# A fused sequence and product-key expert kernel: half of GpSimd's products moved ahead of the weights, two list buffers, the first quad's activations in step 0, and the last norms on VectorE

## What is computed

```
# layer 1: a gated recurrence over the sequence
delta = softplus(x Wdelta'), decay = exp(-delta * sigmoid(log_a))
state_t = decay_t * state_(t-1) + sigmoid(x Wselect') * tanh(x Win')
x = layernorm(x + (sigmoid(x Wgate') * state) Wout')

# layer 2: product-key experts, 8 heads, 2 x 32 keys, 1024 experts
xn = batchnorm(x) * gamma + beta;  q = xn w_q';  sim[p] = q[p] . keys   (p = 0, 1)
sx, ix = top8(sim[0]);  sy, iy = top8(sim[1])
scores, pk = top8(all sums sx + sy);  idx = (32 ix + iy)[pk]
o = gelu(x . key_in[idx]) * softmax(scores)
x = layernorm(x + sum over heads and k of o * key_out[idx])
```

## Time and profile before

| | us |
|---|---|
| median of 3 runs | 490.32 |
| lowest, highest | 487.49, 490.91 |
| the profiled execution: its time | 490.44 |
| the profiled execution: its span | 488.5 |
| DVE busy | 432.3 (88%) |
| PE busy | 359.3 (74%) |
| ACT busy, POOL busy | 245.4, 243.5 (50% each) |

### The profile page before, as it was taken

One profiled execution on the slowest core, in us unless ns is written; L12 is line 12 of the kernel. 1 busy time (PEld: TensorE's weight loads), 2 busy tenths in 40 slices (PEclk: granted clock), 3 DMA queues, 4 the chain that ended last, 5 costly groups with the idle time before them and its releaser, 6 DMA issues.

```text
span 488.5 us, 23430 instructions
## 1 busy us (share of the span) xinstructions
PE 359.3 (74%) x9713; PEld 266.5 (55%) x9713; DVE 432.3 (88%) x2701; ACT 245.4 (50%) x402; POOL 243.5 (50%) x341
## 2 busy tenths in 40 slices
PE   5979858137877778778777887687688778687565
PEld 3445544015545466447655674467356747487555
DVE  2458986999999869999999999989999999999993
ACT  2897664354555534364556445545464456242233
POOL 1023350453529461828382969262929483969030
PEclk9979956767595977797599768877797598867579
DMA  8900000000000000000000000000000000000001
GB/s 241 192 3 1 1 1 0 1 1 3 4 2 5 3 3 4 5 2 5 25 5 3 3 26 3 5 3 26 3 4 4 25 5 3 4 26 4 3 25 44
DMA packets 7658, 8.90 MB, mean 18 GB/s; under 512 B 896, under 2 KB 6912, under 8 KB 7424
## 3 DMA queue, kind: packets, MB, share of 16 engines
q1 hardware_dynamic: 6976, 7.34, 5.8%
q10 hardware_dynamic: 576, 0.07, 0.1%
HBM read 5.31 MB, written 2.10 MB: 15 GB/s over the span
## 4 chain that ended last, share of the span: by engine, by line
DVE 37%; PE 29%; issue 12%; POOL 5%; ACT 3%; DVEq 0%; ACTq 0%; POOLq 0%
PE psum L993 10%; DVE idx L659 7%; PE psum L946 7%; PE psum L980 6%; DVE vals L651 5%; DVE picked L684 5%; DVE arena L718 5%; DVE arena L714 4%; PE psum L926 4%; DVE arena L708 3%; POOL arena L308 2%; DVE top L665 2%; PE psum L918 1%; DVE words L672 1%; POOL code L278 1%
## 5 line engine op out<-in xcount | busy, mean ns | idle before, releaser
L946 PE MATMUL psum<-arena 64*64 64x16 f16 x7424 | 88.3, 182 | 61.0 <-issue 55.3
L946 PEld LDWEIGHTS psum<-arena 64*64 64x64 f16 x7424 | 81.2, 120 | 79.1 <-issue 73.6
L993 PE MATMUL psum<-ko,arena 64*128 64x128 f32 x1024 | 92.2, 358 | 1.9 <-issue 1.9
L993 PEld LDWEIGHTS psum<-ko,arena 64*128 64x128 f32 x1024 | 88.8, 269 | 2.9 <-issue 2.5
L659 DVE FIND_INDEX8 idx<-vals,sims 128x8 uint32<-128x32 f32 x512 | 82.6, 186 | 0.0
L714 DVE TENSOR_TENSOR arena<-iota,listsT 128x4096 f16<-128x4096 f16 x32 | 75.5, 2359 | 0.0
L980 PE MATMUL psum<-x1T,trn 128*64 128x256 f32 x512 | 65.6, 410 | 13.1 <-ACT arena L461 12.4
L308 POOL TENSOR_TENSOR arena<-arena 128x512 f32<-128x512 f32 x56 | 69.6, 1276 | 0.0
L980 PEld LDWEIGHTS psum<-x1T,trn 128*64 128x64 f32 x512 | 35.1, 146 | 49.7 <-ACT arena L461 25.4
L256 POOL TENSOR_TENSOR cand<-vals 128x128 f32<-128x128 f32 x16 | 9.4, 587 | 104.5 <-DVE vals L651 104.5
L453 ACT ACTIVATE arena<-psum 128x1024 f32<-128x1024 f32 x29 | 29.5, 1017 | 60.8 <-PE psum L946 60.8
(11 more groups left out here) (126 smaller groups left out, 570.2 us busy)
## 6 DMA issues: line engine op xcount, KB each, us to landing
x<-in_L_attn_x_dram SPq DMA_DIRECT2D x8, 256.0 KB, 5.6
out_dram<-nat SPq DMA_DIRECT2D x7, 256.0 KB, 2.5
ko<-in_L_ffn_key_out_dram SPq DMA_DIRECT2D x2, 512.0 KB, 9.9
nat<-in_L_ffn_key_in_dram SPq DMA_DIRECT2D x2, 256.0 KB, 10.1
nat<-in_L_ffn_keys_dram SPq DMA_DIRECT2D x2, 128.0 KB, 5.5
out_dram<-nat SPq DMA_DIRECT2D x2, 128.0 KB, 1.7
nat<-in_L_attn_W_delta_dram SPq DMA_DIRECT2D x1, 64.0 KB, 2.8
nat<-in_L_attn_W_in_dram SPq DMA_DIRECT2D x1, 64.0 KB, 2.7
```

Source lines behind the costliest of these rows:

```text
L946: end = pe.matmul(psum[64 * e:64 * e + 64, at:at + NJ], hotx[rows, g, :, e], hotw[rows, part, g, :, e], start=(part == 0), stop=(part == 1))
L993: end = pe.matmul(y2[:, e, m % 2] if m < NS - 1 else y_last[:, e], gl[rows, m % GL, j, :], ko[rows, j, :], start=(j == 0), stop=(j == NJ - 1))
```

## The change

1. `weigh(m - 3)` on POOL is cut in two: its first two instructions stand between candidate_sums(m) and weights(m - 1), the other two stay behind weights(m - 1).
2. listsT has two buffers, used in turn; the copy into it waits for the one-hot matrices of two steps ago instead of those of the last step.
3. The first quad's expert inputs and gelus, of which 2 of 8 rounds stood ahead of step 0 on PE and the rest in step 1, move forward: round 0 on PE between the transposes of chunks 5 and 6, round 1 before scores(0), the rest behind scores(1), which is itself moved ahead of the step loop. On ACT gelus 0 to 3 stand before sims_out(1), gelus 4 and 5 behind it, 6 and 7 in step 1. signs(0) stands ahead of normed(2).
4. The last two parts' norm is one DVE instruction per 128 tokens (subtract the mean, multiply by the reciprocal deviation) instead of a DVE scale and an ACT activation.
5. In the tail DVE takes both_parts(1) before the statistics of the last but one quad, and POOL's last multiplication (L325) waits for one half less of the one-hot matrices (`hot_done` 31 instead of 32).

```diff
--- before.py
+++ after.py
@@ -117,7 +117,7 @@
-        listsT = sb("listsT", [P, 2, 4, P // 2], F16)
+        listsT = sb("listsT", [P, 2, 2, 4, P // 2], F16)
@@ -300,24 +300,26 @@
-            def weigh(m):
+            def weigh(m, first=0, last=4):
                 wait(pool, "p_evac", m * 2 + 2)
                 wait(pool, "gelu_done", (m // 2 + 1) * JR)
-                for r in range(4):
+                for r in range(first, last):
                     js = slice(4 * r, 4 * r + 4)
                     pool.tensor_tensor(gl[:, m % GL, js], pn[:, m % 3, js], gl[:, m % GL, js],
                                        ALU.mult).then_inc(s["a_done"], 1)
 
             for m in range(NS):
                 candidate_sums(m)
+                if m >= 3:
+                    weigh(m - 3, 0, 2)
                 if m >= 1:
                     weights(m - 1)
                 if m >= 3:
-                    weigh(m - 3)
+                    weigh(m - 3, 2, 4)
                 candidate_codes(m)
                 over_eighth(m)
             weigh(NS - 3)
-            pool.wait_ge(s["hot_done"], 2 * NS)
+            pool.wait_ge(s["hot_done"], 2 * NS - 1)
             pool.wait_ge(s["p_evac"], LAST)
@@ -440,8 +442,8 @@
             def lists_out(m):
                 wait(act, "lists_mm", m + 1)
-                wait(act, "hot_done", m * 2)
-                act.activation(listsT[:, :, :, :].rearrange("p h f t -> p f h t"),
+                wait(act, "hot_done", m * 2 - 2)
+                act.activation(listsT[:, m % 2].rearrange("p h f t -> p f h t"),
                                b_lists.rearrange("p (f h t) -> p f h t", f=4, h=2), ACT.Copy).then_inc(s["lists_evac"], 1)
@@ -452,10 +454,10 @@
-            def gelus(q):
+            def gelus(q, first=0, last=JR):
                 wait(act, "y2_mm", q * 2 - 4)
-                for r in range(JR):
-                    if r == 2:
+                for r in range(first, last):
+                    if r == 2 and q > 0:
                         signs(GELU_STEP[q])
@@ -482,17 +484,12 @@
-            def norm_out_half(u):
...
             normed(0)
             sims_out(0)
             normed(1)
+            gelus(0, 0, 4)
+            sims_out(1)
+            gelus(0, 4, 6)
             for m in range(NS):
...
                 low_halves(m)
+                if m == 0:
+                    signs(0)
...
-                if m + 1 < NS:
+                if 1 <= m < NS - 1:
                     sims_out(m + 1)
                 if m + 2 < NS:
                     normed(m + 2)
-                if m in GELU_STEP:
+                if m == GELU_STEP[0]:
+                    signs(m)
+                    gelus(0, 6)
+                elif m in GELU_STEP:
                     gelus(GELU_STEP.index(m))
...
             for u in range(2):
                 spread2_half(u)
-                norm_out_half(u)
@@ -801,13 +802,16 @@
-            def last_scales(u):
+            def last_out(u):
                 n = slice(2 * u, 2 * u + 2)
                 dve.wait_ge(s["sd2"], NCH + u)
                 dve.reciprocal(rstd2[:, n], rstd2[:, n]).then_inc(s["rstd2_done"], 1)
                 dve.wait_ge(s["rstd2_done"], NCH + u)
-                dve.scalar_tensor_tensor(out=nmr2[:, n], in0=mv2[:, n, 0], scalar=-1.0, in1=rstd2[:, n],
-                                         op0=ALU.mult, op1=ALU.mult).then_inc(s["nmr2_done"], 1)
+                dve.wait_ge(s["stored"], 16 * (NCH - 1))
+                for t in range(2 * u, 2 * u + 2):
+                    end = dve.tensor_scalar(outb[:, t, :], zf[:, t, :], mv2[:, t:t + 1, 0], rstd2[:, t:t + 1],
+                                            ALU.subtract, ALU.mult)
+                end.then_inc(s["out_done"], 1)
@@ -826,13 +830,13 @@
             both_parts(0)
             residual(NCH - 2)
+            both_parts(1)
             stats(NCH - 2)
-            both_parts(1)
             both_parts(2)
             scales(NCH - 2)
             for u in range(2):
                 last_residual(u)
-                last_scales(u)
+                last_out(u)
@@ -913,6 +927,11 @@
+                if c == 6:
+
+                    pe.wait_ge(s["x1T_evac"], 1)
+                    pe.wait_ge(s["w_evac"], 5)
+                    experts_in(0, 0, 1)
                 wait(pe, "bst_done", c + 1 - RING)
@@ -994,9 +1003,10 @@
-            pe.wait_ge(s["w_evac"], 5)
-            experts_in(0, 0, 2)
+            experts_in(0, 1, 2)
             scores(0)
+            scores(1)
+            experts_in(0, 2)
             for m in range(NS):
...
-                if m + 1 < NS:
+                if 1 <= m < NS - 1:
                     scores(m + 1)
-                if m in GELU_STEP:
-                    experts_in(GELU_STEP.index(m), 2 if m == GELU_STEP[0] else 0)
+                if m in GELU_STEP[1:]:
+                    experts_in(GELU_STEP.index(m))
```

More of the change, by code:

```diff
@@ L483, in spread2_half @@
                 act.activation(rstd2[:, n], mv2[:, n, 1], ACT.Sqrt, bias=eps[:, 0:1]).then_inc(s["sd2"], 1)
-            def norm_out_half(u):
-                act.wait_ge(s["nmr2_done"], NCH + u)
-                act.wait_ge(s["stored"], 16 * (NCH - 1))
-                for t in range(2 * u, 2 * u + 2):
-                    end = act.activation(outb[:, t, :], zf[:, t, :], ACT.Identity, bias=nmr2[:, t:t + 1],
-                                         scale=rstd2[:, t:t + 1])
-                end.then_inc(s["out_done"], 1)
             normed(0)
@@ L518, in _ @@
                     spread2(m // 2 - 2)
-                if m < NS - 1 and m not in GELU_STEP:
+                if 0 < m < NS - 1 and m not in GELU_STEP:
                     signs(m)
@@ L703, in spread @@
                 def spread(f, n):
-                    v = listsT[:, hf, f, :].rearrange("p (g s) -> p g s", s=2)
+                    v = listsT[:, m % 2, hf, f, :].rearrange("p (g s) -> p g s", s=2)
                     return v.unsqueeze(2).to_broadcast([P, 32, n, 2])
@@ L716, in hots_of @@
                 wait(dve, "hoty_done", m * 2 + hf + 1)
-                both = listsT[:, hf, 2:4, :].rearrange("p w (g s) -> p (w g) s", s=2).unsqueeze(2)
+                both = listsT[:, m % 2, hf, 2:4, :].rearrange("p w (g s) -> p (w g) s", s=2).unsqueeze(2)
                 dve.tensor_tensor(hotw[:, :, at].rearrange("p w g j s -> p w (g j s)"),
@@ L907, in _, with experts_in @@
                 weights(g)
+            def experts_in(q, first=0, last=JR):
+                tokens = x1T[:, q * CW:(q + 1) * CW].rearrange("d (m e p) -> d e m p", m=2, e=2)
+                for r in range(first, last):
+                    wait(pe, "gelu_done", q * JR + r - 1)
+                    for b in range(2):
+                        for e in range(2):
+                            end = pe.matmul(b_g[r % 2][64 * e:64 * e + 64, b * SW:(b + 1) * SW],
+                                            trn[:, 9 + r, 64 * b:64 * b + 64], tokens[:, e], start=True, stop=True)
+                    end.then_inc(s["g_mm"], 1)
             for c in range(NCH):
@@ L972, in quarters @@
                     end.then_inc(s["q_mm"], 1)
-            def experts_in(q, first=0, last=JR):
-                tokens = x1T[:, q * CW:(q + 1) * CW].rearrange("d (m e p) -> d e m p", m=2, e=2)
-                for r in range(first, last):
-                    wait(pe, "gelu_done", q * JR + r - 1)
-                    for b in range(2):
-                        for e in range(2):
-                            end = pe.matmul(b_g[r % 2][64 * e:64 * e + 64, b * SW:(b + 1) * SW],
-                                            trn[:, 9 + r, 64 * b:64 * b + 64], tokens[:, e], start=True, stop=True)
-                    end.then_inc(s["g_mm"], 1)
             def experts_out(m):
```

## The result

The changed kernel took 498.01 us (median of 4 runs, 496.42 to 500.02), beside 490.48 us for the kernel before on the same chip (4 runs, 487.49 to 490.91). The ratio is 1.0191, with an interval of 1.0144 to 1.0237: slower, and 1.4 us above the forecast of 496.6. The profiled execution took 499.16 us with a span of 497.4, where before it was 490.44 with 488.5.

A forecast was written before the change was run, and what follows sets the result against it. The kernel was taken as bound by DVE, PE close behind. Start +0.9, steps 3 and 4 -0.8, steps 5 to 14 +6.2, step 15 +1.1, tail -1.15 gave +6.25 on 490.44: 496.7, as median 496.6, range 486 to 501.

The forecast's parts named there:

- The sum: Whole kernel: all terms together add +6.25 us to the profiled 490.44, giving 496.7.
- the ten steps: Steps 5 to 14: DVE's floor rises to 48.96 us a pair and old waits vanish in it, +6.2 us.
- The blocked codes: DVE's L692, steps 3 to 15: waits for POOL's whole second product, 1.1 us a step, bounds nothing to 1.24.
- 14 us or more: Sign over the whole kernel: DVE's busy time would rise by some 14 us or more.
- Rival A: Codes on DVE aren't blocked, or go before the second product; tail's L325 may be harmless: 486.7 us, chance 0.22.
- Rival C: The copy L691 meets the second product and only its rest is paid, 0.3 to 0.5 a step: 491.3 us, chance 0.18.
- Rival B: DVE's new time isn't taken up, as lists and PE's queue come later too: +11 us, 501.5, chance 0.1.
- Steps 3 and 4: Waits in step 4 absorb both steps' 1.1 price; earlier signs start the one-hot matrices 0.8 sooner: -0.8 us.
- The start: Up to step 0: round 0 ahead of the last transposes makes DVE start at 84.65 instead of 83.75, +0.9 us.
- Those margins hold at 2.4 GHz: Steps 0 and 1: gelus, copies and signs(0) end before DVE needs them, signs at 96.1 against 97; no cost.
- The tail: Step 15 and tail: +1.1 us for step 15's price, -1.15 for the tail with the list buffer.
- The turns: Tail: L325's four POOL products alternate with DVE's scale and last three one-hot operations, +2.2 us (0 to 2.6).

The follow-up runs named there:

- The split alone: The kernel before with only two of weigh's four POOL products moved ahead of weights(m - 1): 496.02 us, ratio 1.0124.
- Together: Kernel before with one product ahead, two list buffers, statistics behind, norms on DVE, one ACT norm earlier, scores(0) ahead of round 1: 484.65 us, ratio 0.9881.

## Why the prediction was right, and where it wasn't

**The sum.** The profiled execution took 499.2 us where the sum gave 496.7. Of the some 2.5 us missing, 1.7 are in steps 0 and 1, 0.7 in steps 3 and 4, and 0.3 and 0.2 at the start and in the tail; the ten steps gave 0.3 back. The forecast's +1.3% lies just under the measured interval of +1.4 to +2.4%.

**The blocked codes.** Right in mechanism, place and size: 1.07 us in 11 steps of 13 against 1.1, pairs of 48.85 against 48.96, the ten steps +5.9 against +6.2, DVE's work +15.7 where "14 us or more" was named, its idle time in these steps half gone. That the ten steps agree to 0.3 is luck in part, since the same code took up to 3.5 us less in other executions; the length of the codes and DVE's busy time don't vary so. Of its bounds (nothing to one product, 1.24) the prediction chose by the nearest row, the pack blocked in step 15, and by the order of turns in step 2. The split alone gives the price alone, the order put back takes it away, and one product in place of two takes it away with all else kept. Rival A is out. Rival C's arrangement, the copy meeting the second product, occurred in steps 6 and 12, but at the price of the forecast, about 1.0, since the copy came at the product's start and not at its end. Rival B, that the waits don't take anything up, would have made the split alone some 11 us slower; it is 1.24% slower (0.9 to 1.6%, or 4.3 to 7.9 us), so B is out for two products. DVE's idle time in the ten steps, 3.5 and 4.0 with two products against 4.6 to 8.1, agrees. With four products or with the codes moved, time is lost in just such waits.

**Steps 3 and 4.** -0.8 was forecast and -0.1 came. The waits for words went, but that for the lists shrank only from 4.00 to 3.62, and the one-hot matrices of step 4 started 0.1 sooner and not 0.8. By itself the split gave -0.3. With one product ahead they start 1.0 to 2.6 sooner (39.91, 40.70 and 41.49 us after the start of step 3), so the second product takes most of this gain away; by which path wasn't tried.

**The start.** The sum was near (+0.9 against +1.2), but by terms that made up for each other: here xn was ready 1.16 later and not 1.84, the first scores started 0.5 later and not 1.1, and the slower clock added 0.7 where 0.2 was to be saved. Executions differ at this place: xn was ready between 79.94 and 81.87 us in nine with no round ahead of the last transposes, and at 82.18, 82.80, 83.05 and 83.57 in the four with round 0 ahead of them; on average the shift is 1.7, near the forecast's 1.84. The term that failed is "Those margins hold at 2.4 GHz", entered at nothing: the prediction had the clock of 1.2 GHz as an aside to rival B, at up to 2.7, and it should have been in the sum. PE was granted 1.2 GHz in the scores of both steps, the signs came 1.35 late, and steps 0 and 1 took 1.7 more. A sign of it was at hand: PE had no gap ahead of the old scores, and by the prediction's own times the change opens one. But the gap alone doesn't decide. In the last kernel above (Together), PE stood idle for 1.96 and the scores took 1.98, at 2.4 GHz. Nor is the clock low in every execution of this edit: with one product ahead in the changed kernel the scores ran at 1.2 GHz only up to the end of the first, the second took 1.98, and the signs were in time. In the three executions where the signs were late, the second scores took 3.78. What sets the clock here stays open; round 0 behind the transposes changed the gap and the lateness together.

**The tail.** The sum was right (0.1 against -0.05), its terms less so. From the start of step 15 to the tail's first scales (the reciprocal just before L745) 0.1 was gained, where +1.1 - 0.72 - 0.9 makes a gain of 0.5. The turns cost 1.6 and not 2.2. The wait of 0.73 for ACT's norm wasn't in the prediction; with it the stretch between the two pairs of scales took 0.6 more, beside the turns. From the second such reciprocal to the end it is 1.9 shorter, with the waits of 1.72 and 0.47 in it, where 1.2 + 0.55 were forecast. The new waits stand behind ACT's norms or a store: by making the residuals earlier, the edit ran them into buffers not yet free.

The parts by themselves add up to 1.24 + 0.6 - 0.63 = +1.2%, and together they make +1.9% (1.4 to 2.4). Some of the rest lies in the start: in four executions of the same edit there, step 0 began at 84.64, 84.97, 85.84 and 86.36 (82.79 to 84.44 in seven with the start of before), and the signs were late in three of them. Whether that is all of it stays open.

## What to carry to other kernels

Before an instruction stream is moved into a gap of POOL, look at what DVE issues in that gap: an operation that reads two tiles in SBUF and queues up against a queued POOL product waits for all of it. An idle gap holds as many products as end before that operation is issued, and here that was one and not two, a difference of about 2%. When a tail is made earlier on one engine, list who frees the buffers that it will write: here the residual made earlier ran into a wait for ACT's norm that hadn't been visible. And before a gain of some us is read off one trace, look at what the same code takes in other executions: here the ten steps differed by 4 us with nothing changed in POOL's order. Three edits brought 0.6 us of trace there; the kernel that also takes that norm earlier, with other changes beside it, had a tail 3.2 us shorter than the one without.

## What the runs showed of the hardware

The turns between DVE and POOL aren't strict. With all four products ahead, a POOL instruction of 64 elements that had started 0.02 us before a DVE operation sat out three in a row, and none of them was slowed. Timeline of that execution:

```profile
231.91 4.21 POOL L277 TENSOR_TENSOR code<-ixf,iyf 128x64 f32<-128x64 f32 x1
231.93 0.67 DVE L710 TENSOR_TENSOR arena<-iota,listsT 128x1024 f16<-128x1024 f16 x1
232.52 2.28 DVE L716 TENSOR_TENSOR arena<-iota,listsT 128x4096 f16<-128x4096 f16 x1
234.72 1.22 DVE L720 TENSOR_TENSOR arena<-arena,listsT 128x2048 f16<-128x2048 f16 x1
```

A copy of 16-bit numbers with one input was blocked too (0.31 to 1.26 and 1.39). The Trainium skill ("SBUF — State Buffer", section "Who interferes with whom") has the loser blocked for the whole instruction, which the 1.07 us that the codes lose beside a product of 1.24 bear out; which of two waiting ones goes next is shown only by these rows. And a gap of idle ahead of a short piece of work doesn't by itself say at what clock it runs: after 1.90 us of idle PE's four scores took 3.78 at 1.2 GHz, after 1.96 us in the kernel under Together they took 1.98 at 2.4, as after 1.14 us in the one with round 0 behind the transposes.
